# Issuing the fourth convolution tap load from POOL's queue instead of SP's

## The chip, the cores and the metric

The kernel runs on one core of a Trainium2 chip. The metric is the device time of one execution in microseconds (us); less is better. Each time stands for a whole execution, from the first instruction to the last store.

## The reference

Two blocks follow each other, each with a residual. `x` is 32 batches of 64 channels by 1024 positions, in float32.

```python
# block 1
c1 = conv_general_dilated(x, L0_cond_weight, (1,), padding=[(4, 4)], feature_group_count=4)   # 9 taps, 4 groups
c1 = c1 + (cond_128 @ L0_cond_c_weight.T)[:, :, None] + fside_S_0[None, :, None]
y  = einsum('bsd,od->bso', c1, L0_ffn_weight) + L0_ffn_bias
y += where(batch uses an adapter, (c1 @ A[adapter].T) @ B[adapter].T, 0)      # three LoRA adapters of rank 16
x  = x + y
# block 2
h   = gelu(gelu(cond_128 @ W0 + b0) @ W1 + b1)
att = softmax(h @ W2 + b2)                                   # over 8 experts
m   = einsum('boi,bih->boh', einsum('bk,koi->boi', att, weight), x) + (att @ bias_k)[:, :, None]
G   = softmax over the top 16 of 64 scores m @ Wr.T
x   = x + ((m @ A.T) * G) @ B.T * 2                          # 64 rank-16 experts, gated
```

## The kernel before, in words

The 32 batches are worked off in four groups of eight. Group 0 has code of its own (`first_group` on each engine), groups 1 to 3 run through `group`. In a group TensorE (PE) does the grouped convolution as matmuls, then the feed-forward product in three-pass split precision (a high and a low part of each operand, L1512 to L1514), the adapters, the mixing and the gated experts. ScalarE (ACT) makes the high parts, VectorE (DVE) the low parts, and GpSimd (POOL) the routing of the adapters and the mixing weights. Synchronisation is written out by hand with semaphores; there is no planner. Each engine's instructions run in the order in which they stand in its block, and a wait holds up all that stands behind it in that block.

Loads come from three places. SP's block issues nearly all of them; ACT's block starts with three (`load_taps(act, 0)`, `load_taps(act, 2)`, and the small constants `consts1`); POOL's block issues DMAs only later, to store adapter rows (L664 to L670) and to gather them (L676).

The convolution weights stand in the tile `toep`, in four parts, one for each group of channels `cg`. `load_taps(eng, cg)` (L313 to L318) loads one part, 128 KB, from overlapping windows of the array `taps`: 8 phases by 16 channels by 256 floats, so one run of 1 KB for each of 128 partitions. Each part has its own semaphore `s_taps[cg]`. Parts 0 and 2 are issued by ACT, parts 1 and 3 by SP. Both queues work side by side; SP's queue starts with the first batch of the padded input (`load_first(0, ...)`, 258 KB), then parts 1 and 3, then the second batch (`load_first(1, ...)`), `hidden_w` (the tile `gate`, 128 KB), the input of the next batches (`load_conv_in`) and the weights.

PE starts with `WARM_UP` = 12 matmuls on the tile `ones`, which it may begin when POOL's first memset (L585, semaphore `s_ones` at 1) is done (L1506 to L1508). A float32 matmul shows as two records, so these are 24 records. Then come the convolutions of the eight batches (L1663 to L1690). For batch 0 PE waits ahead of each group for its own part of the taps (L1673): the four parts are wanted one after the other. A batch is 4 groups by 2 matmuls by 2 records = 16 records of L1526. Behind batch 0 stand `context()` (L1593, needs `consts1`) and `hidden(0)` (L1600, needs `hidden_w`), then batch 1, the spread of the bias (L1681) and so on.

POOL's block starts with four memsets: `ones` (L585), `lora_a_r` (L586), `lora_s2` (L587) and a part of `lora_s2` (L589); then it waits for `consts2` and `starts` (`adapters()`). DVE's block starts with a wait for `s_ones` at 4, all four memsets (L1007), and ACT waits for the same before it fills `lora_a_r` (L863).

Of the kernel before, what the change touches and what calls it, by code (L numbers as in the profile page):

```python
# [70 lines left out]
def adaln_ffn_kernel(nc, conv_x, x, taps, pieces, first_consts, hidden_w, later_consts, lora_a, lora_b,  # L71
                     starts, wr, expand, spread, out):
    with ExitStack() as ctx:
# [41 lines left out]
        gate_x = sb("gate_x", [P, GATES, TOK])  # L115

        consts1 = sb("consts1", [P, sum(w for _, w in FIRST)])
        consts2 = sb("consts2", [P, sum(w for _, w in LATER)])
        starts_i = sb("starts_i", [P, 4], I32)
        starts_f = sb("starts_f", [P, 4])  # L120
# [192 lines left out]
        def load_taps(eng, cg):  # L313


            tap, ci = CI, taps.shape[2] * CI
            windows = bass.AP(taps.tensor, taps.offset + cg * CI * ci, [[tap, PH], [ci, CI], [1, 2 * P]])
            eng.dma_start(toep[:, cg].rearrange("r h n -> r (h n)"), windows).then_inc(s_taps[cg], 16)  # L318
# [14 lines left out]
        def _(sp):  # L333
# [66 lines left out]
            def load_first(b, done):  # L400
                width = CG * (Q + 1)
                sp.dma_start(conv_in[:, b].rearrange("p g q -> p (g q)"),
                             conv_x[0, 0, :, b * width:(b + 1) * width]).then_inc(done, 16)

            load_first(0, s_convin[0])
            load_taps(sp, 1)
            load_taps(sp, 3)
            load_first(1, s_convin_b1)
            sp.dma_start(hidden_stage, hidden_w).then_inc(s_hidden_w, 16)
            load_conv_in(0, 1)  # L410
# [172 lines left out]
        @block.gpsimd  # L583
        def _(pool):
            pool.memset(ones[:, :], 1.0).then_inc(s_ones, 1)  # L585
            pool.memset(lora_a_r[:, :, :].bitcast(F32), 0.0).then_inc(s_ones, 1)  # L586
            pool.memset(lora_s2[:, :].bitcast(F32), 0.0).then_inc(s_ones, 1)  # L587
            pool.wait_ge(s_ones, 3)
# [1358 lines left out]
```

## Time and profile before

| what | value |
|---|---|
| device time, three runs | 651.86, 652.17, 654.58 us (median 652.17) |
| the profiled execution's own time | 652.13 us |
| its span (first to last instruction) | 650.3 us |
| PE busy | 642.3 us, 99% of the span |
| DVE, ACT, POOL busy | 450.8, 214.3, 118.4 us |

The span is 1.83 us shorter than the profiled execution's own time; that remainder lies around the recorded instructions. A time of the profile counts from the start of the span. PE's weight loads (PEld) run beside its matmuls. The end of a matmul is modelled, so that neighbouring matmuls overlap in the timeline; the distance between their starts is the better measure.

### The profile page before, as it was taken

The numbers are of one execution on the slowest core, as the hardware profiler recorded it, in microseconds if no ns is written. First come the engines' busy times: TensorE is split into PE (matmuls) and PEld (weight loads), VectorE is DVE, ScalarE is ACT, GpSimd is POOL, SyncE is SP. The second block draws the span as 40 slices with busy tenths as digits, with TensorE's granted clock in tenths as the row PEclk, the third lists the DMA queues.
The fourth block names the chain that finished last, engine by engine and source line by source line (L and its number), as shares of the span: only waits on it lengthen the run. The fifth ranks groups of instructions, "written<-read, shape, count | busy, mean of one in ns | idle before, by whom it ended". The sixth has DMA issues, their size and how long they took to land.

```text
span 650.3 us, 8392 instructions
## 1 busy us (share of the span) xinstructions
PE 642.3 (99%) x3176; PEld 533.3 (82%) x3176; DVE 450.8 (69%) x695; ACT 214.3 (33%) x278; POOL 118.4 (18%) x143
## 2 busy tenths in 40 slices
PE   9999999999999998999999999999999999999997
PEld 8878888888897887888889788888889888888885
DVE  2858469649378888548869848727967957665685
ACT  2714135334143124335114312324422421333420
POOL 1499750000000257000000127300000020000000
PEclk9999999999999999999999999999999999999999
DMA  8586844985978966786985795277797676038695
GB/s 304 215 292 255 334 140 143 359 259 206 402 236 346 398 229 255 259 242 227 370 293 201 296 367 180 101 224 255 269 338 263 263 262 247 15 119 217 205 342 221
DMA packets 54570, 164.94 MB, mean 254 GB/s; under 512 B 6756, under 2 KB 7652, under 8 KB 54544
## 3 DMA queue, kind: packets, MB, share of 16 engines
q1 hardware_dynamic: 46240, 148.05, 63.1%
q10 hardware_dynamic: 5328, 9.61, 4.7%
q0 software_dynamic: 2976, 6.95, 3.4%
q8 instruction: 13, 0.21, 0.1%
q14 instruction: 13, 0.11, 0.0%
HBM read 138.23 MB, written 26.36 MB: 253 GB/s over the span
## 4 chain that ended last, share of the span: by engine, by line
PE 94%; DVE 3%; DMA 2%; ACT 0%; ACTq 0%; issue 0%; DVEq 0%; SPq 0%
PE bank L1512 25%; PE bank L1514 25%; PE bank L1513 25%; PE bank L1526 9%; PE bank L1557 3%; PE bank L1533 2%; DMA piece_lo<-kept 1%; DVE u_lo L1142 1%; PE bank L1563 1%; PE bank L1564 1%; DMA toep<-taps 1%; PE bank L1545 1%; DVE v_lo L1019 1%; DVE work L1062 1%; PE bank L1549 0%; PE bank L1551 0%
## 5 line engine op out<-in xcount | busy, mean ns | idle before, releaser
L1013 DVE TENSOR_TENSOR piece_lo<-raw,piece_hi 128x1024 fp32r<-128x1024 f32 x60 | 73.1, 1223 | 84.3 <-ACT piece_hi L751 84.3
L1512 PE MATMUL bank<-piece_hi,u_hi 128*128 128x512 f32 x272 | 107.8, 396 | 0.1
L1514 PE MATMUL bank<-piece_hi,u_lo 128*128 128x512 f32 x272 | 107.4, 395 | 0.0
L1513 PE MATMUL bank<-piece_lo,u_hi 128*128 128x512 f32 x272 | 107.3, 394 | 0.0
L751 ACT ACTIVATE piece_hi<-raw 128x1024 fp32r<-128x1024 f32 x60 | 63.3, 1058 | 129.2 <-PE bank L1514 86.9
L1512 PE MATMUL bank<-v_hi,piece_hi 128*128 128x512 f32 x256 | 101.7, 397 | 0.0
L1514 PE MATMUL bank<-v_hi,piece_lo 128*128 128x512 f32 x256 | 101.1, 395 | 0.0
L1513 PE MATMUL bank<-v_lo,piece_hi 128*128 128x512 f32 x256 | 101.1, 395 | 0.0
L1512 PE MATMUL bank<-piece_hi,v_hi 128*128 128x512 f32 x192 | 75.8, 395 | 0.1
L1514 PE MATMUL bank<-piece_hi,v_lo 128*128 128x512 f32 x192 | 75.8, 395 | 0.0
L1513 PE MATMUL bank<-piece_lo,v_hi 128*128 128x512 f32 x192 | 75.7, 395 | 0.0
L756 ACT ACTIVATE u_hi<-work 128x512 fp32r<-128x512 f32 x64 | 40.1, 631 | 88.9 <-DVE work L1118 52.0
L1055 DVE TENSOR_TENSOR x<-x,bank 128x512 f32<-128x512 f32 x86 | 54.4, 681 | 16.6 <-PE bank L1545 8.3
L1512 PEld LDWEIGHTS bank<-piece_hi,u_hi 128*128 128x128 f32 x272 | 51.2, 188 | 12.4 <-issue 0.6
L1514 PEld LDWEIGHTS bank<-piece_hi,u_lo 128*128 128x128 f32 x272 | 51.2, 188 | 11.9
L1513 PEld LDWEIGHTS bank<-piece_lo,u_hi 128*128 128x128 f32 x272 | 51.2, 188 | 11.8
L1526 PE MATMUL bank<-toep,conv_in 128*128 128x128 f32 x512 | 59.1, 276 | 0.6 <-DMA toep<-taps 0.6
L1526 PEld LDWEIGHTS bank<-toep,conv_in 128*128 128x128 f32 x512 | 58.1, 192 | 1.2 <-DMA toep<-taps 0.8
L1514 PEld LDWEIGHTS bank<-v_hi,piece_lo 128*128 128x128 f32 x256 | 48.2, 188 | 11.3
L1513 PEld LDWEIGHTS bank<-v_lo,piece_hi 128*128 128x128 f32 x256 | 48.2, 188 | 11.0
L1512 PEld LDWEIGHTS bank<-v_hi,piece_hi 128*128 128x128 f32 x256 | 48.2, 188 | 11.0
L1019 DVE TENSOR_TENSOR u_lo<-work,u_hi 128x512 fp32r<-128x512 f32 x64 | 43.7, 689 | 15.3 <-ACT u_hi L756 14.0
(178 smaller groups left out, 831.5 us busy)
## 6 DMA issues: line engine op xcount, KB each, us to landing
raw<-pieces SPq DMA_DIRECT2D x76, 512.0 KB, 5.8
piece_hi<-kept SPq DMA_DIRECT2D x48, 512.0 KB, 5.2
piece_lo<-kept SPq DMA_DIRECT2D x48, 512.0 KB, 6.1
x<-x SPq DMA_DIRECT2D x16, 512.0 KB, 5.4
gate_x<-gates ACTq DMA_DIRECT2D x32, 256.0 KB
out<-x SPq DMA_DIRECT2D x32, 256.0 KB, 4.7
conv_in<-conv_x SPq DMA_DIRECT2D x15, 516.0 KB, 7.4
conv_in<-pieces SPq DMA_DIRECT2D x12, 512.0 KB, 9.6
```

The lines of the kernel that those rows point to most:

```text
L751: act.activation(piece_hi[:, n % SLOTS, :], raw[:, r % RAWS, :], ACT.Copy).then_inc(s_piece_hi, 1)
L756: act.activation(to, of, ACT.Copy).then_inc(s_hi, 1)
L1013: dve.tensor_tensor(piece_lo[:, n % SLOTS, :], raw[:, r % RAWS, :], piece_hi[:, n % SLOTS, :].bitcast(F32), ALU.subtract).then_inc(s_piece ...
L1019: dve.tensor_tensor(to, of, hi, ALU.subtract).then_inc(s_lo, 1)
L1055: dve.tensor_tensor(half, half, of, ALU.add).then_inc(done, 1)
L1062: dve.tensor_tensor(work[:, c, :], banks[bank][:, :], mixb_bc[:, :, :].rearrange("p b c -> p (b c)"), ALU.add).then_inc(s_item, 1)
L1512: pe.matmul(to, left_hi, right_hi, start=first, stop=False)
L1513: pe.matmul(to, left_hi, right_lo, start=False, stop=False)
L1514: return pe.matmul(to, left_lo, right_hi, start=False, stop=last)
L1526: mm = pe.matmul(banks[bank][:, cg * P:(cg + 1) * P], conv_in[:, b, cg, h:h + Q], toep[:, cg, 1 - h, :], start=(h == 0), stop=(h == 1))
L1533: mm = pe.matmul(banks[bank][0:LORA_M, :], lora_a_r[:, k, :], part[:, k, :], start=(k == 0 and part is u_hi), stop=(k == NCH - 1 and part ...
L1557: mm = pe.matmul(banks[bank][:, t * P:(t + 1) * P], x1[:, t, c * P:(c + 1) * P], blockdiag[:, t, :], start=True, stop=True)
```

## The change

One call leaves SP's block, and the same call for the same part goes into POOL's block behind the first memset. The destination, the source and the semaphore stay the same.

```diff
             load_first(0, s_convin[0])
             load_taps(sp, 1)
-            load_taps(sp, 3)
             load_first(1, s_convin_b1)
             sp.dma_start(hidden_stage, hidden_w).then_inc(s_hidden_w, 16)
             load_conv_in(0, 1)
@@
         @block.gpsimd
         def _(pool):
             pool.memset(ones[:, :], 1.0).then_inc(s_ones, 1)
+            load_taps(pool, 3)
             pool.memset(lora_a_r[:, :, :].bitcast(F32), 0.0).then_inc(s_ones, 1)
             pool.memset(lora_s2[:, :].bitcast(F32), 0.0).then_inc(s_ones, 1)
             pool.wait_ge(s_ones, 3)
```

## Rows read from the trace of the kernel before

**Rows 1.** The page: engines' busy time, and PE and its clock in 40 slices.
```profile
PE 642.3 (99%) x3176; PEld 533.3 (82%) x3176; DVE 450.8 (69%) x695; ACT 214.3 (33%) x278; POOL 118.4 (18%) x143
...
PEclk9999999999999999999999999999999999999999
```
**Rows 2.** Waits of PE in the whole span: line, waited for, us, times, longest.
```profile
PE bank L1563 <- DVE v_lo L1019: 2.2, 3, 1.3
PE bank L1508 <- POOL ones L585: 1.0, 1, 1.0
PE bank L1526 <- DMA toep<-taps: 0.6, 1, 0.6
```
**Rows 3.** Chain that ended last, 0 to 10 us: start, length, what.
```profile
0.75 1.22 ACTq L318
1.97 0.03 issue
2.00 5.16 DMA toep<-taps
7.16 0.04 issue
7.20 1.16 PE bank L1526 x8
8.36 0.21 PE bank L1593 x2
8.57 0.34 PE bank L1600 x2
```
**Rows 4.** Timeline from 0.7 us: start, length, engine, line, operation, tiles, count.
```profile
0.74 0.20 POOL L585 MEMSET ones<- 128x128 f32 x1 [0.29 <-POOLq L1937]
0.74 0.39 SPq L402 DMA_DIRECT2D conv_in<-conv_x  x1
0.88 0.85 POOL L586 MEMSET lora_a_r<- 128x896 f32 x1
1.19 1.43 SPq L318 DMA_DIRECT2D toep<-taps  x2
2.25 0.52 POOL L589 MEMSET lora_s<- 32x512 f32 x1
2.65 0.47 ACTq L745 DMA_DIRECT2D consts<-first_consts  x1
2.67 0.48 SPq L402 DMA_DIRECT2D conv_in<-conv_x  x1
3.19 0.43 SPq L409 DMA_DIRECT2D gate<-hidden_w  x1
5.55 1.06 PE L1526 MATMUL bank<-toep,conv_in 128*128 128x128 f32 x8
8.72 0.22 DVE L1149 TENSOR_SCALAR ctx_t<-bank,consts 64x8 f32<-64x8 f32 x1 [8.72 <-PE bank L1593]
```
**Rows 5.** Line L318, the tap loads: duration ns min/median/max, first and last start.
```profile
L318 SPq DMA_DIRECT2D toep<-taps x2: 606/689/772, 1.2 to 2.0; - x2
```
**Rows 6.** DMA issues, 0 to 10 us: count, KB each, median us to landing.
```profile
conv_in<-conv_x SPq DMA_DIRECT2D x2, 258.0 KB, 4.2
consts<-first_consts ACTq DMA_DIRECT2D x1, 153.5 KB, 5.3
gate<-hidden_w SPq DMA_DIRECT2D x1, 128.0 KB, 5.2
```
**Rows 7.** Windows: length, busy of PE, PEld, DVE, ACT, POOL, clock, DMA share, GB/s.
```profile
2.00:2.50 0.50, 0.50 (x5) 0.50 (x4) 0.00 (x0) 0.00 (x0) 0.44 (x2) 1.00 0.79 301
3.00:3.50 0.50, 0.50 (x4) 0.50 (x3) 0.00 (x0) 0.00 (x0) 0.00 (x0) 1.00 0.52 180
4.00:4.50 0.50, 0.50 (x4) 0.50 (x4) 0.00 (x0) 0.00 (x0) 0.00 (x0) 1.00 0.98 259
6.00:6.50 0.50, 0.50 (x6) 0.42 (x4) 0.00 (x0) 0.00 (x0) 0.00 (x0) 1.00 0.97 254
```
**Rows 8.** POOL's first DMA, then all its DMAs on `lora_rows` with their landing times.
```profile
78.35 0.90 POOL L664 DMA_DIRECT2D lora_rows<-lora_m  x1 [2.96 <-PE bank L1551]
...
L676 POOL DMA_INDIRECT lora_m<-lora_rows,lora_row x12: 945/948/1954, 89.3 to 393.6; - x12
L668 POOL DMA_DIRECT2D lora_rows<-lora_m x2: 512/515/518, 81.0 to 84.4; - x2
...
DMA to landing us min/median/max: 2.5/3.6/7.9
```
**Rows 9.** Line L664, POOL's six direct stores of 96 KB: their landing times.
```profile
DMA to landing us min/median/max: 2.7/3.0/3.1
```
**Rows 10.** Longest idle time in front of a DMA issued by POOL with no releaser shown.
```profile
89.28 1.08 POOL L676 DMA_INDIRECT lora_m<-lora_rows,lora_row  x1 [3.33 <-issue]
```
**Rows 11.** DVE's and ACT's work ahead of the first feed-forward product.
```profile
18.10 0.69 DVE L1023 TENSOR_TENSOR work<-bank,cond_bc 128x512 f32<-128x512 f32 x1 [0.50 <-PE bank L1526]
21.22 0.63 ACT L756 ACTIVATE u_hi<-work 128x512 fp32r<-128x512 f32 x1 [0.81 <-DVE work L1023]
23.74 0.19 ACT L856 ACTIVATION_READ_ACCUMULATOR att<-bank,attstat 32x1 f32 x1
24.00 0.19 PEld L1512 LDWEIGHTS bank<-piece_hi,u_hi 128*128 128x128 f32 x1 [0.26 <-issue]
```

## The prediction

> **What bounds the kernel now.** I read the page first. PE is busy for 642.3 of 650.3 us [rows 1], so all its idle time together is 8.0 us, 1.2% of the span, and no change to the loads can give more than that. The waits of PE come next [rows 2]: the reader sees one wait on the taps, 0.6 us, once. The 1.0 us ahead of the warm-up matmuls waits for the memset of ones, which the change leaves in front. So what the change can touch is the opening, and there the chain [rows 3] shows the order: ACT issues its first tap load at 0.75 us (1.22 us long), its second, part 2, at 2.00 us, that one lands 5.16 us later, at 7.16, and PE goes on at 7.20. The part that PE waits for is thus part 2, on ACT's queue, and not part 3, the one that is moved. PE's first eight convolution records (parts 0 and 1) end at 5.55 + 1.06 = 6.61 us [rows 4]; 7.20 - 6.61 = 0.59 us is the whole stall. Parts 2 and 3 then run as eight records in 1.16 us with no gap between: part 3 is wanted at 7.20 + 0.58 = 7.78 us and was there.
>
> **Part by part.** (a) *SP loses an issue.* SP's two tap issues take 1.43 us together, one of them 0.61 and one 0.77 [rows 4, 5]. SP's next load starts at 2.67 us; without the second tap issue it starts about 0.65 us sooner (a middle of the two), and so does all behind it in the opening. The second batch (issue 2.67) and hidden_w (issue 3.19, landing 5.2 later = 8.39) profit [rows 4, 6]. PE wants hidden_w at 8.57 [rows 3], so this load had 0.2 us to spare; sooner by up to 0.65 it does not become the next wait. Alone this is worth nothing, because PE waits for none of them today; it is the cover for a gain elsewhere.
>
> (b) *POOL gains an issue.* It starts when the memset of ones is done, 0.74 + 0.20 = 0.94 us, or at 0.88, where the next memset starts now [rows 4]. The trace has no load of 128 runs by POOL. The nearest rows: a direct DMA of little data takes POOL 0.51 us, its very first one (48 rows) 0.90, a gather of 128 rows 0.95 and once 1.95 [rows 8]. I take 0.95, since 128 runs for 128 partitions is the shape of the gather; ends 0.5 and 1.95. From start to landing POOL's DMAs take 2.5, 3.6 in the middle and 7.9 us at most [rows 8]; the six direct stores among them 2.7 to 3.1 [rows 9]. With the middle part 3 lands at 0.9 + 3.6 = 4.5 us; ends 3.4 and 8.8. It is wanted at 7.78 us, or, if the stall goes, at 6.61 + 0.58 = 7.19: 2.7 us to spare in the middle. Queued behind the issue on POOL are three memsets that end at 2.25 + 0.52 = 2.77 us now and at 3.7 then (4.7 at most). DVE waits for them, but its first work starts at 8.72 us, released by PE [rows 4]; the cover is 4 us and the cost is 0. Uncovered it would be 0.95 us.
>
> (c) *Part 2, which decides.* Its issue on ACT's queue does not move. What moves is who shares the DMA engines with it. Their share is 0.79 at 2.0 to 2.5 us and 0.52 at 3.0 to 3.5, but 0.98 and 0.97 at 4.0 and 6.0 us [rows 7]: in the second stretch they have no room left. Part 3 is issued by SP in the same moment as part 2 by ACT (both near 2.0 us) and shares the full stretch with it. Issued at 0.9 us by POOL it falls mostly into the stretch with room. Its 128 KB at the 254 GB/s of 6.0 to 6.5 us are 0.5 us of all the engines; if all of that is taken out ahead of part 2, part 2 lands at 6.66, and the stall is 0.05. Against it stands that SP's queue does not stay empty: the second batch, 258 KB, moves up by 0.65 us into the same place, twice the bytes. If it costs part 2 as much as part 3's going gives, nothing is won; if it costs twice that, part 2 lands 0.5 us later and 0.5 us are lost. So (c) lies between +0.5 us and -0.54 us.
>
> A gain has a cap. consts1, issued by ACT behind part 2 at 2.65 us, lands 5.3 later, at 7.95 [rows 4, 6]; PE wants it at 8.36 [rows 3]. It has 0.41 us to spare, so if its landing does not move too, PE can be sooner by 0.4 us and no more. I take 0.3 us for (c), below the cap, because both loads on ACT's queue lose the same rival. Does such a gain last to the end? The next place where PE nearly waits is the first feed-forward product at 24.00 us: ACT's exponential is done at 23.74 + 0.19 = 23.93, just ahead [rows 11]. But ACT had waited 0.81 us for DVE there, and DVE 0.50 us for PE's convolution, so this chain moves with PE. Behind it PE has no wait on a load, and 2.2 us on DVE in the whole rest [rows 2].
>
> The sum against the profiled execution: 652.13 (span 650.3 and 1.83 around it) + 0 (a) + 0 (b) - 0.3 (c) = 651.8 us. The median of the runs is 652.17, 0.04 more, so 651.9 is what I expect of a median.
>
> The trace shows POOL's DMAs landing after 2.5 us at best [rows 8]. The Trainium skill, "DMA: Bandwidth & Descriptors", section "Anatomy of one DMA — SWDGE (gpsimd) path", gives about 2.0 us plus bytes over 436 GB/s for one; the estimate by it is 2.3 us for part 3, a landing at 3.2 instead of 4.5, and the sum stays as it is.
>
> **The rivals.** *Same bytes, same landing (A).* Part 2 lands at 7.1 to 7.3 as before, since SP's moved-up loads fill what part 3 left. For it: 258 KB come for 128 KB, and the share stays near 1. Against it: the 128 KB do find room at 2 to 4 us. Time 652.1 to 652.2. The Trainium skill, same page, section "Issuing engines are not separate DMA queues", says that DMAs of all issuing engines interleave on the same 16 and that a second issuer saves only issue time; by that rule this rival is the result.
>
> *Part 2 lands later (B).* The same mechanism with the other sign, 0.1 to 0.5 us: 652.3 to 652.7. For it: the second batch moves up, and POOL's queue is a third one that wants its turn beside parts 0 and 1. Against it: part 3 leaves just where part 2 is served.
>
> *POOL's load is late (C), the slow side.* Place: PE at L1526, ahead of the last four records of batch 0. It decides from a landing at 7.2 to 7.8 us on. At the longest landing in the trace, 7.9 us, part 3 comes at 8.8 and PE loses 8.8 - 7.78 = 1.0 us: 653.2. If POOL's first DMA has a start-up of its own as long as the longest unexplained gap in front of one, 3.33 us [rows 10], it comes at 12.1 and costs 4.4 us: 656.5. For it: a DMA on POOL in the first microsecond is nowhere in the trace. Against it: POOL's first DMA took 0.90 us, only 0.4 more than the later small ones, and no direct store of its took over 3.1 us to land [rows 9]; the longer ones are gathers. The Trainium skill, "GPSIMD Engine Reference", section "Instruction dispatch", speaks of about 6 us ahead of the first call to freshly loaded GpSimd code; the estimate with it would be a landing at 10.5 and 2.7 us lost. The trace's first DMA on POOL shows no such gap in itself.
>
> *The load is wanted and comes, but PE's clock differs (D)* is no rival of its own: the granted clock is full in every slice [rows 1] and in each window of the opening [rows 7], through a stall of 0.59 us; a shorter stall leaves it so.
>
> **How the numbers follow.** Forecast (0.1 to 0.6 us faster) 0.50; A 0.25; B 0.12; C 0.11, of which 0.04 for the long start-up; 0.02 for a gain beyond the opening by a shift of later waits that no row shows. The likeliest gives 651.9. Its own range is 651.5 to 652.1. The three runs lie 2.7 us apart, more than all of this, so for eight in ten I go from 651.0 (all of the stall gone and some scatter) to 653.4 (C at the trace's longest landing, or scatter upwards). A measurement of this kernel tells a change from none at about 0.5%, 3.3 us. Faster than that needs five times the stall: 0.02. Slower needs the long start-up: 0.04. The rest, 0.94, is within.
>
> **What would show it.** Right: SP's load of the second batch starts near 2.0 us; POOL shows a DMA_DIRECT2D of about 0.95 us from 0.9; the wait of PE L1526 on the taps shrinks from 0.6 to 0.2 to 0.4, still on ACT's part 2; DVE's first operation comes about 0.3 us sooner than 8.72. Wrong: the chain runs through a tap load on POOL (C), or the ACT load lands at 7.2 or later (A, B), or PE now waits ahead of L1593 for consts1. A difference of over 1 us would mean that something outside the opening moved, and that my reading of PE as bound by its own work from 24 us on fails.

## The result, and the profile after

The changed kernel is slower: 655.26 us median (653.22 to 660.46, 20 runs) against 652.68 us (651.46 to 654.58, 20 runs), a ratio of 1.005 with a 95% interval of 1.0035 to 1.0064 (the ratios here go by all the runs and not by the two medians, whose ratio is 1.004). The forecast of 651.9 us, and its range up to 653.4, missed it. Not only the middle moved: 9 of the 20 runs lie above 656 us, where the kernel before has none. The granted clock of each run, as a mean over the whole execution, splits the 20 runs in two halves: the ten at 0.999 or 1.000 lie between 653.22 and 655.07 us (median 654.34), the ten at 0.992 to 0.997 between 655.45 and 660.46 (median 657.92). About 1.7 us of the loss are thus there at full clock; the rest comes with a lower one.

The profiled execution took 656.92 us (span 655.1, against 652.13 and 650.3); with a mean granted clock of 0.997 it belongs to the second half. The waits of PE in the whole span (line, waited for, us, times, longest) answer to [rows 2]:

```profile
PE bank L1526 <- DMA toep<-taps: 2.9, 2, 1.7
PE bank L1563 <- DVE v_lo L1019: 2.2, 3, 1.3
PE bank L1508 <- POOL ones L584: 1.0, 1, 1.0
PE bank L1593 <- DMA consts<-first_consts: 0.5, 1, 0.5
```

The wait on the taps has grown from 0.6 to 2.9 us, a wait for consts1 has come up, and the rest of the kernel waits as before (2.2 us on DVE in both). The timeline of PE, 4 to 16 us, shows where (start, length, count, and in brackets the idle time before it):

```profile
5.37 0.61 PE L1526 MATMUL bank<-toep,conv_in 128*128 128x128 f32 x4
7.18 0.71 PE L1526 MATMUL bank<-toep,conv_in 128*128 128x128 f32 x4 [1.20 <-DMA toep<-taps]
9.55 1.16 PE L1526 MATMUL bank<-toep,conv_in 128*128 128x128 f32 x8 [1.66 <-DMA toep<-taps]
11.16 0.39 PE L1593 MATMUL bank<-consts 128*64 128x8 f32 x2 [0.45 <-DMA consts<-first_consts]
11.92 3.30 PE L1526 MATMUL bank<-toep,conv_in 128*128 128x128 f32 x16
```

Four records a group: the first gap is in front of the second group, so part 1 (SP's) is late, at 7.18 us, where PE had it without a wait at about 6. The second gap is in front of the third group: part 2 (ACT's) comes at 9.55 instead of 7.20 [rows 3]. The third and fourth group then run together, so part 3, the load that was moved, kept nobody waiting. The stalls are 1.20 + 1.66 + 0.45 = 3.31 us, against 0.59. Batch 1 starts at 12.11 us in the chain instead of 8.91, and lasts 3.12 us instead of 1.87:

```profile
2.65 8.47 DMA consts<-first_consts
11.16 0.39 PE bank L1593 x2
11.54 0.57 PE bank L1600 x2
12.11 3.12 PE bank L1526 x16
```

The timelines of POOL and of SP, and the DMA issues of the first 10 us (count, KB each, us to landing), answer to [rows 4] and [rows 6]:

```profile
1.31 0.83 POOL L318 DMA_DIRECT2D toep<-taps  x1 [0.37 <-issue]
2.13 0.88 POOL L586 MEMSET lora_a_r<- 128x896 f32 x1
```
```profile
2.03 0.41 SPq L402 DMA_DIRECT2D conv_in<-conv_x  x1
2.48 0.43 SPq L408 DMA_DIRECT2D gate<-hidden_w  x1
2.95 0.96 SPq L338 DMA_DIRECT2D conv_in<-conv_x  x2
```
```profile
consts<-first_consts ACTq DMA_DIRECT2D x1, 153.5 KB, 8.5
toep<-taps POOLq DMA_DIRECT2D x1, 128.0 KB, 6.7
gate<-hidden_w SPq DMA_DIRECT2D x1, 128.0 KB, 7.2
```

POOL's load starts at 1.31 us, takes 0.83 and lands at about 8.0. SP's second batch starts 0.64 us sooner, and the first large loads 0.72 us sooner (L338, 2.95 us; before, they started at 3.67). consts1, issued at the same 2.65 us as before, lands 8.5 us later instead of 5.3; hidden_w 7.2 instead of 5.2.

The packets of 4 to 5 us by queue (q1 is SP's, q10 ACT's, q0 POOL's; packets, MB, share) show what each queue moves there. First the kernel before:

```profile
q10 hardware_dynamic: 117, 0.13, 46.6%
q1 hardware_dynamic: 113, 0.14, 46.3%
```

and the changed one, in which ACT's queue, the one with part 2, moves nothing in that microsecond:

```profile
q1 hardware_dynamic: 108, 0.15, 53.9%
q0 software_dynamic: 35, 0.05, 15.2%
```

Last, PE's clock. The windows (length, busy time of PE, PEld, DVE, ACT, POOL, granted clock, DMA share, GB/s) show half the full clock for a stretch behind the stalls:

```profile
5.00:7.00 2.00, 0.98 (x9) 0.79 (x8) 0.00 (x0) 0.00 (x0) 0.00 (x0) 1.00 1.03 307
7.00:9.00 2.00, 0.71 (x4) 0.52 (x4) 0.00 (x0) 0.00 (x0) 0.00 (x0) 1.00 1.08 319
12.00:13.00 1.00, 1.00 (x6) 1.00 (x6) 0.63 (x1) 0.76 (x2) 0.00 (x0) 0.50 1.04 403
15.00:17.00 2.00, 2.00 (x12) 0.94 (x11) 0.00 (x0) 0.60 (x1) 0.00 (x0) 1.00 1.03 413
```

### The profile page after: what moved, and what is told of

Same layout as the page of the kernel before. It is cut to its first block, busy times and chain, and to the rows that moved or that the text cites. A ratio compares the mean times of both kernels' runs of the same rounds, so it can differ in the third digit from the quotient of the medians.

```text
span 655.1 us, 8392 instructions
## 1 busy us (share of the span) xinstructions
PE 644.6 (98%) x3176; PEld 534.3 (82%) x3176; DVE 450.9 (69%) x695; ACT 214.4 (33%) x278; POOL 119.6 (18%) x144
## 4 chain that ended last, share of the span: by engine, by line
PE 95%; DVE 3%; DMA 1%; ACTq 0%; DVEq 0%; issue 0%
PE bank L1512 25%; PE bank L1514 25%; PE bank L1513 25%; PE bank L1526 9%; PE bank L1557 4%; PE bank L1533 2%; DMA consts<-first_consts 1%; DVE u_lo L1142 1%; PE bank L1563 1%; PE bank L1564 1%; DVE v_lo L1019 1%; PE bank L1545 1%; DVE work L1062 1%; PE bank L1549 0%; PE bank L1551 0%; ACTq L318 0%
## 5 line engine op out<-in xcount | busy, mean ns | idle before, releaser
L1526 PE MATMUL bank<-toep,conv_in 128*128 128x128 f32 x512 | 60.6, 280 | 2.9 <-DMA toep<-taps 2.9
L1526 PEld LDWEIGHTS bank<-toep,conv_in 128*128 128x128 f32 x512 | 59.5, 195 | 3.6 <-DMA toep<-taps 3.2
```

Source lines behind the costliest of these rows:

```text
L1526: mm = pe.matmul(banks[bank][:, cg * P:(cg + 1) * P], conv_in[:, b, cg, h:h + Q], toep[:, cg, 1 - h, :], start=(h == 0), stop=(h == 1))
```

## The experiments

Three theories were put to the test in turn. P: POOL's DMA itself holds back the other loads. S: SP's queue, moved up by one issue, does. K: the clock lost behind the stall makes the long runs. S was later split into L (it is the large loads) and F (it is the second batch). "b1" below is the start of batch 1 in the chain of the experiment's profile (8.91 us in the kernel before, 12.11 in the changed one). It is read from one execution and moves more than the medians do: e2 has it 1.9 us later at a median only 0.9 us higher. The ratio is to the kernel before on the same chip; each verdict below goes by it.

**e1_no_part3.** SP moved up, no POOL load.
```diff
-            load_taps(sp, 3)
-                                   toep[:, cg, 1 - h, :], ...
+                                   toep[:, min(cg, 2), 1 - h, :], ...      # and no wait for part 3
```


> The kernel before without the load of part 3 anywhere: SP's queue moves up by the one issue as in the changed kernel, POOL issues nothing. The convolution of the fourth channel group uses part 2's weights, so part 3's 128 KB are left out. Theory P (POOL's DMA itself holds back the loads of SP and ACT): no stall beyond part 2's, which lands at 7.2 us or sooner; time as the kernel before or up to 0.6 us less. Theory S (SP's loads, moved up by 0.6 us, push back parts 1 and 2 and consts1): part 2 lands at 9 us or later, PE loses 3 to 4 us, time 2 to 3 us above the kernel before.


Measured: 653.56 us (652.34 to 655.62), ratio 1.0012 (1.0000 to 1.0024), b1 8.88. PE had no stall on a load in its profile, but its first convolution record starts at 6.12 us there, behind the warm-up, and at 5.55 us in the kernel before [rows 4]; that can hide a stall of 0.6 us. S by itself, with 128 KB less to move, is worth 0.1%, not 0.5%, where S had said 2 to 3 us and P a time as before or shorter.

**e2_extra_pool** and **e3_small_pool.** The kernel before with an extra load on POOL, of 128 KB (e2) or 4 KB (e3).
```diff
             pool.memset(ones[:, :], 1.0).then_inc(s_ones, 1)
+            load_extra(pool)        # e3: load_extra(pool, 8); part 3's windows into gate_x[:, 3, 0:width]
```


> The kernel before, whole, with part 3 still on SP, and one extra load of the same 128 KB issued by POOL behind the memset of ones into a place that nothing reads (the tile gate_x). SP's and ACT's queues are as before. Theory P: ACT's queue moves nothing for about a microsecond around 4 to 5 us, parts 1 to 3 and consts1 land 2 to 3 us later, time 2 to 4 us above the kernel before. Theory S: 128 KB more in the opening cost 0.5 us at most, time within 0.7 us of the kernel before.

> As the kernel with the extra load on POOL, but each of the 128 runs is 32 bytes instead of 1 KB: 4 KB in all, as many runs. If POOL's DMA hurts by its bytes or by its share of the DMA engines' time: time as the kernel before. If it hurts by the act of a software-generated DMA beside the others (its descriptors, its turn on each engine): 2 to 4 us above it, as with 128 KB. Theory S: as the kernel before.


Measured: e2 653.85 us, ratio 1.0021 (1.0010 to 1.0033), b1 10.81; e3 652.98 us, ratio 1.0000 (0.9991 to 1.0009), b1 9.64. The act of a POOL DMA (e3) costs nothing that can be measured; 128 KB more in the opening, moved by POOL (e2), cost 0.2%. P's picture did come true in e2's profile: ACT's queue has no packet from 4 to 5 us, and part 2 lands 7.05 us after its issue instead of 5.16 [rows 3], with SP's queue in its old order:

```profile
2.00 7.05 DMA toep<-taps
```

But the time rose by 0.9 us in the median, where P said 2 to 4.

**e4_sp_keeps** and **e8_sp_small.** The changed kernel with a load left in part 3's old place on SP, of 128 KB (e4) or 4 KB (e8).
```diff
             load_taps(sp, 1)
+            load_extra(sp)          # e8: load_extra(sp, 8)
             load_first(1, s_convin_b1)
```


> The changed kernel (part 3 on POOL), with a load of the same 128 KB left in SP's queue in part 3's old place, into a tile that nothing reads. SP's issues stand at their old times. Theory S: the loss is gone, time within 0.7 us of the kernel before. Theory P: the loss stays, 2 to 4 us above the kernel before, as in the kernel with the extra load on POOL; the two differ only in which of the two copies PE waits for.

> The changed kernel (part 3 on POOL), with a load of 4 KB in 128 runs of 32 bytes in part 3's old place in SP's queue, into a tile that nothing reads. SP's later loads are thus issued at their old times, without part 3's bytes. With 128 KB in that place the loss was 0.1 to 0.7 us. If the time of the second batch's issue is what matters: as there or less, 0 to 0.7 us above the kernel before. If the order of bytes matters and not the time: 2 to 3 us above it, as the changed kernel.


Measured: e4 653.10 us, ratio 1.0011 (0.9998 to 1.0024), b1 10.44; e8 652.45 us (651.58 to 654.05), ratio 0.9999 (0.9990 to 1.0008), b1 9.32. This settles the larger part: with part 3 on POOL, as in the change, one issue of 4 KB on SP takes the whole loss away. SP's timeline of e8:

```profile
2.01 0.61 SPq L324 DMA_DIRECT2D gate_x<-taps  x1
2.66 0.46 SPq L408 DMA_DIRECT2D conv_in<-conv_x  x1
3.17 0.42 SPq L415 DMA_DIRECT2D gate<-hidden_w  x1
3.63 0.43 SPq L344 DMA_DIRECT2D conv_in<-conv_x  x1
```

The 0.61 us of the issue is what counts, not what it carries: with 128 KB in it (e4), which are 128 KB more in all, the kernel loses 0.1%, an interval that overlaps both e8's and e2's. So POOL's own 128 KB, in place of SP's, cost nothing once SP's loads stand at their old times.

**e9_bulk_held, e12_hold_after, e11_hold_before.** Which of SP's loads came too soon: the 4 KB issue behind hidden_w (e9), or a wait there until part 2 has landed, in the changed kernel (e12) and in the kernel before (e11).
```diff
             sp.dma_start(hidden_stage, hidden_w).then_inc(s_hidden_w, 16)
+            load_extra(sp, 8)                   # e9
+            sp.wait_ge(s_taps[2], 16)           # e11, e12
             load_conv_in(0, 1)
```


> The changed kernel, with the 4 KB load not in part 3's old place but behind hidden_w: SP's second batch and hidden_w are issued 0.65 us sooner than in the kernel before, the large loads (input of batches 2 and on, weights) at their old times. Theory L (the loss comes from the large loads, let in 0.65 us sooner beside part 2 and consts1): time as the kernel before, within 0.7 us. Theory F (it comes from the second batch, which takes part 2's turn on the 8 engines that carry the taps): 2 to 3 us above it.

> The changed kernel with the same wait of SP behind hidden_w. Theory L: the whole loss goes, time within 0.5 us of the kernel before or below it, like the kernel before with the hold. Theory F: part 2 still lands at 8.5 us or later, 1.5 to 3 us above the kernel before.

> The kernel before, with SP waiting behind hidden_w until part 2 has landed, before it issues the large loads. Theory L: part 2 lands at about 6.2 us, consts1 at 7, PE begins batch 1 at 8.0 to 8.5 instead of 8.9 us, time 0.3 to 0.9 us below the kernel before; the large loads come 2 to 2.5 us later, which the rows of the profile cover (PE wants batch 2 at 12.3 us, now landed at 9.9). Theory F: no gain, within 0.3 us; or a loss if the cover of a later load is shorter than it looks.


Measured: e9 653.24 us, ratio 1.0008 (0.9997 to 1.0019), b1 9.96; e12 653.56 us, 1.0007 (0.9997 to 1.0016), b1 9.50; e11 652.73 us, 0.9999 (0.9988 to 1.0010), b1 9.27. L holds for the changed kernel: in e9 the second batch and hidden_w stay moved up, only the large loads are held back to their old times (3.61 us), and most of the loss goes. Not all of it: e12 stands 0.7 us above the kernel before in the median, where L said 0.5 or less. The landings in e9 (us to landing; changed kernel 8.5, 6.7, 7.2):

```profile
consts<-first_consts ACTq DMA_DIRECT2D x1, 153.5 KB, 5.8
toep<-taps POOLq DMA_DIRECT2D x1, 128.0 KB, 4.7
gate<-hidden_w SPq DMA_DIRECT2D x1, 128.0 KB, 5.5
```

But L forecast a gain for e11, and there is none. In its profile PE waits for no load, and it is the warm-up that binds; the chain of e11:

```profile
1.00 5.49 PE bank L1509 x24
6.49 2.19 PE bank L1527 x16
```

In the profile of before PE's first convolution record already starts at 5.55 us [rows 4]. A stall of 0.6 us that only shows when the warm-up is quick is hardly a gain to be had. Nor does the hold bring part 2 back: the chains of e9 and e12 have it 6.21 and 5.75 us after its issue, the kernel before 5.16 [rows 3], the changed one 9.55 - 2.00 = 7.55:

```profile
2.00 6.21 DMA toep<-taps
...
8.25 1.16 PE bank L1534 x8
```
```profile
2.00 5.75 DMA toep<-taps
...
7.79 1.16 PE bank L1527 x8
```

In both, ACT's queue has no packet from 4 to 5 us, as in the changed kernel. That empty microsecond is not the loss by itself: e1 has 18 packets in it, e8 has 8 and e10 none, and none of them has the changed kernel's loss; from 5 to 6 us ACT's queue then moves 172, 164 and 162 packets in these three, against 79 in the changed kernel. In e9 it moves only 35 from 5 to 6 us, and 164 from 6 to 7. So a part of part 2's delay, up to 1 us, stays while the second batch is moved up and POOL moves 128 KB; e2 shows such a delay without the first of the two, so F is not shown as its cause. The large loads add the rest and nearly all of consts1's.

**e10_up_small.** e1 with e3's small POOL load.
```diff
-            load_taps(sp, 3)
+            load_extra(pool, 8)     # behind the memset of ones; the fourth group as in e1
```


> SP moved up, part 3's 128 KB left out (the fourth group uses part 2's weights), and POOL issues a load of only 4 KB in 128 runs behind the memset of ones. With no POOL load this stood 0.1% above the kernel before, with POOL's 128 KB it is the changed kernel, 0.5% above. If POOL's bytes are the other half of the loss: 0 to 0.8 us above the kernel before. If it is the act of a POOL DMA beside a moved-up SP: 2 to 3 us above.


Measured: 653.42 us, ratio 1.0007 (0.9997 to 1.0017), b1 10.32. SP moved up and a POOL DMA of few bytes are as harmless together as apart. The whole loss appears only with both the moved-up large loads and POOL's 128 KB; either alone is worth 0.1% (e1, e10) and 0.0 to 0.2% (e8, e2). Whether the two merely add up the intervals do not say: 0.1 and 0.2% against 0.50% (0.35 to 0.64) and, in e15 below, 0.37% (0.18 to 0.56).

**e6_act** and **e7_late.** Other places for part 3: on ACT behind part 2, and on POOL behind all four memsets.
```diff
             load_taps(act, 2)
+            load_taps(act, 3)       # e6, POOL's is gone
```
```diff
             pool.wait_ge(s_ones, 4)
+            load_taps(pool, 3)      # e7, instead of behind the first memset
```


> Part 3 on ACT's queue behind part 2 instead of on POOL: SP's queue is moved up as in the changed kernel, all 128 KB are loaded, POOL issues nothing. Theory S (moving SP up costs by itself): part 2 starts a microsecond later than before, consts1 lands after 9 us since it stands behind one more load, time 1 to 2.5 us above the kernel before. Theory P (only POOL's DMA costs): within 0.7 us of the kernel before, less a late consts1.

> The changed kernel with POOL's load behind all four memsets instead of the first, so 1.5 us later. If POOL's DMA does its harm by standing in the stretch in which ACT's part 2 and SP's next load are started (3.5 to 5 us), part 1 and part 2 land as before (4.7 and 7.2 us), but part 3 itself comes at 8 to 9 us: one stall of about 1 us instead of two, time 0.5 to 1.5 us above the kernel before. If it harms whenever it comes: 2 to 3 us above.


Measured: e6 657.81 us (655.25 to 661.96), ratio 1.0094 (1.0062 to 1.0126), b1 13.25; e7 656.92 us (654.71 to 662.54), ratio 1.0081 (1.0049 to 1.0112), b1 11.26. Both are worse than forecast. In both PE stands still for two us or so ahead of the fourth group; here part 3 is what is late. POOL issues nothing in e6, so a loss of this kind does not need POOL; but part 3 and consts1 stand further back on ACT's queue there, and e6 does not separate that from SP's moved-up loads. This is PE in e6, then in e7:

```profile
7.81 0.71 PE L1526 MATMUL bank<-toep,conv_in 128*128 128x128 f32 x4 [0.40 <-DMA toep<-taps]
10.85 0.71 PE L1526 MATMUL bank<-toep,conv_in 128*128 128x128 f32 x4 [2.33 <-DMA toep<-taps]
```
```profile
7.34 0.71 PE L1526 MATMUL bank<-toep,conv_in 128*128 128x128 f32 x4 [0.88 <-DMA toep<-taps]
10.00 0.71 PE L1526 MATMUL bank<-toep,conv_in 128*128 128x128 f32 x4 [1.95 <-DMA toep<-taps]
11.10 3.63 PE L1526 MATMUL bank<-toep,conv_in 128*128 128x128 f32 x16
```

e7's last row is batch 1, for the most part at half clock, and its runs reach 662.5 us.

**e5_warm, e13_fill, e14_fill_before, e15_after_again.** The clock: more warm-up, or 8 matmuls ahead of the wait for part 2, in the changed kernel and in the kernel before; and the changed kernel again.
```diff
-WARM_UP = 12
+WARM_UP = 26                        # e5
```
```diff
                         if b == 0:
+                            if cg == 2:
+                                for _ in range(8):
+                                    pe.matmul(banks[7][:, 0:P], ones[:, :], ones[:, :], start=True, stop=True)
                             pe.wait_ge(s_taps[cg], 16)
```


> The changed kernel with 26 warm-up matmuls instead of 12, so that PE has work until about 8.4 us and idles little before the late taps. In the profile of the changed kernel PE's clock was granted at half from 11.2 us on, behind its stalls, and batch 1 took 3.12 us instead of 1.87. Theory K (the clock lost behind the stall makes the upper tail): no stretch at half clock after the first 6 us, no run above 656.5, highest and lowest within 2.5 us, median 654.3 to 655.0. Rival (the tail is late loads alone): the spread of the changed kernel stays, 653 to 660.

> The changed kernel with 8 more matmuls on ones (16 records, about 1.8 us at full clock) for batch 0 behind the second channel group, ahead of the wait for part 2, where PE would idle. Theory K (the clock lost behind the stall makes the tail): full clock in the profile from 6 us on, no run above 656.5 us, median 653.8 to 654.8, which is below the changed kernel although work was added. Rival (late loads alone): median as the changed kernel or up to 0.5 us above, and runs to 658 us and more.

> The kernel before with the same 8 matmuls: the price of the fillers where part 2 lands at 7.2 us. Fillers run from 6.6 to 8.4 us, the stall of 0.6 us is inside: both theories say 1.0 to 1.4 us above the kernel before, with a spread as small as its.

> The changed kernel once more, on the same chip as the two with fillers. Both theories: 2 to 3.5 us above the kernel before, runs spread over 4 us or more. Theory K: if its profiled run is above 656 us, there is a stretch of half clock between 9 and 15 us in it; if it is below 655, there is none.


Measured: e5 656.70 us (655.17 to 658.08), ratio 1.0066 (1.0049 to 1.0083); the warm-up ran until 9.36 us, past every part's landing, and cost more than it saved. K's numbers for e5 failed (median 654.3 to 655.0, no run above 656.5; three of its six runs are above that), though the granted clock of all six is 0.999 or 1.000, so it was the added work and not the clock. e13 655.28 us (654.72 to 656.17, 5 runs), ratio 1.0043 (1.0030 to 1.0056); e14 654.39 us (653.49 to 655.77), 1.0029 (1.0019 to 1.0040), 1.8 us above the kernel before where 1.0 to 1.4 was forecast; e15 654.80 us (653.72 to 660.21, 10 runs), 1.0037 (1.0018 to 1.0056). e15's profiled run is its second slowest, 658.86 us, and its windows and its chain show why; half clock in a profile above 656 us is what K had forecast:

```profile
9.00:11.00 2.00, 1.22 (x9) 1.03 (x9) 0.00 (x0) 0.03 (x1) 0.00 (x0) 0.92 1.00 396
15.00:17.00 2.00, 2.00 (x5) 0.67 (x3) 0.00 (x0) 0.00 (x0) 0.00 (x0) 0.50 1.02 410
17.00:20.00 3.00, 3.00 (x14) 2.26 (x14) 1.70 (x3) 1.23 (x2) 1.74 (x6) 0.50 0.46 184
```
```profile
11.89 3.57 PE bank L1526 x16
15.47 2.00 PE bank L1681 x2
```

Batch 1 and the spread of the bias take 3.57 and 2.00 us instead of 1.87 and 1.05: 2.65 us in these two lines, at half clock, from a b1 (11.89) that is even earlier than in the first profile. With work in the gap (e13) the clock is full throughout; windows of e13:

```profile
7.00:9.00 2.00, 1.82 (x16) 1.63 (x16) 0.00 (x0) 0.00 (x0) 0.00 (x0) 1.00 1.05 386
11.00:13.00 2.00, 2.00 (x19) 1.88 (x18) 0.86 (x2) 1.13 (x2) 0.00 (x0) 1.00 1.03 396
```

and no run is above 656.2. K holds for the long runs. Beside the five runs of e13 the granted clock of every run bears it out: in the changed kernel and in e15 every run above 655.2 us has 0.991 to 0.997 and every one below it 0.998 or more, and no run of the kernel before that was taken beside the experiments has less than 0.999. The profiles fit too: half clock shows in the changed kernel, e15, e6 and e7, where PE had stood still for 2.8 to 3.5 us in all, and in no other. Its forecast that the median would fall below the changed kernel's did not come true (655.28 against 654.80): the fillers cost 1.8 us in the kernel before, and half of the changed kernel's runs keep their clock without them.

## Why the prediction was wrong

*(a), SP loses an issue: the times were right, the worth was wrong.* SP's loads started 0.64 us sooner, as said. I called that a cover, worth nothing either way. I followed only the two loads that PE wants, and not the 516 KB loads behind them, which PE wants much later and which moved up as well. e8 and e9 show them to be the larger half of the loss: with them at their old times 0.50% shrinks to 0.08% (e9). The issue of part 3 had been a brake in SP's queue.

*(b), POOL's issue: nearly right.* 0.83 us against 0.95; it started at 1.31 instead of 0.94 because of 0.37 us that no row of before showed. It landed 6.7 us after its start, inside the range of 2.5 to 7.9 [rows 8], and rival C (POOL's load late) did not occur: PE reached part 3 at about 10.1 us, 2 us behind its landing. The three memsets behind it cost nothing. The prediction's other estimate, 2.3 us to landing, was 4.4 us short, and of the long start-up that C allowed for only those 0.37 us appeared. What I took for granted is that part 3's bytes would pass in the stretch with room: of the 80 packets of POOL's queue, 35 moved between 4 and 5 us. By themselves they are harmless even so (e8); on top of part 3 on SP they cost 0.2% (e2).

*(c), part 2: the step that failed.* I put it between +0.5 and -0.54 us, from one sum of bytes over the mean rate. Part 2 came 2.35 us later (9.55 against 7.20), and the term as a whole measured about 3.2 us at b1, 0.4 of it the lower clock on L1593 and L1600. That profile is one of the longer runs; over the runs at full clock the term is 1.7 us, over all of them, with the clock, 2.6 (medians). Rival B had the sign and, in part, the mechanism, at 0.1 to 0.5 us; its size was out by a factor of three (full clock) to six (the profile). The reason can be read in three places. The measure: I took the DMA share, a mean over 16 engines, as the room that there is. It was down to 0.69 from 4 to 5 us (0.93 in the kernel before), with ACT's queue moving nothing and part 2 waiting all the same; in e15's profile it was 0.95 there, with ACT's queue just as empty. The share does not tell whether a given load gets its turn. The company: I counted the second batch as what comes in for part 3, and not the large loads behind it; with those held back part 2 landed 5.75 to 6.21 us after its issue (e12, e9) instead of 7.55. And the price was bound by part 2 alone, where part 1 (1.20 us of stall) and consts1 (0.45 us) were as exposed; consts1 had 0.41 us to spare, which I had worked out only as a cap on a gain.

*The clock: dismissed, and it made the tail.* I wrote that the clock stays since a shorter stall leaves it so; that held only if the stall got shorter. In both profiles of the changed kernel half clock followed the three stalls of together 3.3 us, worth 1.25 us on batch 1 and 0.4 us ahead of it in the first and 2.65 us on two lines in the second. Ten of the twenty runs have a mean granted clock below 0.999. The range had no room for it.

*The bound of the whole* was right: nothing outside the opening moved. PE's wait on DVE is 2.2 us in both. The rule of the Trainium skill that I weighed for rival A ("DMA: Bandwidth & Descriptors", "Issuing engines are not separate DMA queues": a second issuer saves only issue time) agrees with what POOL's load gave SP, 0.64 us of issue time. The time saved did harm here. Rival A itself, part 2 at 7.1 to 7.3 us, did not occur.

What stays open: why ACT's queue is empty, or nearly so, from 4 to 5 us whenever SP's second batch or a small load is issued beside part 2 (e1, e8, e9, e10), or POOL moves 128 KB beside SP's old order (e2, e4). The DMA share in that microsecond is 0.68 to 1.00 in these profiles, so it explains nothing. The experiments show that it happens, not how the queues share the engines, and not why ACT's queue makes up for it in e1, e8 and e10 and not in the changed kernel. Nor is each share exact: the effects of e1, e2, e9 and e12 are 0.5 to 1.4 us with intervals of about 0.7 us to each side. No version beat the kernel before.

## What to carry to other kernels

In this kernel one issue less on a queue moved large loads in front of small ones. When an issue is taken off a queue, follow everything behind it, the loads that nobody wants yet above all: moved up, they compete with the small loads that the start hangs on. An issue, or a wait, ahead of the first large load is a brake worth keeping (e8, e12), though in the kernel before, which has such a brake, a longer one gained nothing (e11). And price a stall of the tensor engine in the opening twice, once for itself and once for the clock that it may lose behind it.

## What the runs showed of the hardware that was not expected

- A POOL DMA of 128 KB took 4.5 to 6.9 us to land in the crowded opening (e12, e7), one of 4 KB 4.3 and 3.7 us (e3, e10); in the quiet stretch of before, 96 KB took 2.7 to 3.1 [rows 9].
- 0.37 us lie between POOL's memset and its DMA with no releaser shown.
- The 24 warm-up records ended between 5.3 and 6.5 us from one profile to another (e15, e11), with nothing to wait for in them. In e14 they took 5.49 us, 0.23 us each, and the 16 records of the same matmul ahead of the third group 1.79 us, 0.11 us each. The granted clock reads 1.00 in both stretches, so that column does not show the slower one; neither could [rows 7].
- An issue takes SP 0.61 us for 128 runs of 32 bytes, as for 128 runs of 1 KB.
- The kernel before itself varies by 3.5 us (651.25 to 654.76 in 35 runs), about six times the stall that this change aimed at.
